# Another opening for a fused attention and mixture-of-experts kernel: two projection tiles first, weight groups centred beside the heads, zero products in TensorE's gaps

## What is computed

```python
qkv = jnp.einsum('bsh,oh->bso', x, w_qkv)            # x is already normalised
...
q = _layernorm(q, qn_g, qn_b)
k = _layernorm(k, kn_g, kn_b)
q = q * cos + _rotate_half(q) * sin
k = k * cos + _rotate_half(k) * sin
...
scores = jnp.einsum('bhqd,bhkd->bhqk', q, k) / jnp.sqrt(jnp.float32(D))
weights = jax.nn.softmax(jnp.where(causal, -jnp.inf, scores), axis=-1)
...
x = x + _layernorm(attention(_layernorm(x)), axis=-1)
x = x + _layernorm(experts(_layernorm(x)), axis=-1)
```

## Time and profile before

| | |
|---|---|
| median of 3 runs | 674.17 us (672.75 to 674.7) |
| the profiled execution's own time | 673.56 us |
| its span in the trace | 671.8 us |
| busy: PE, weight loads, DVE, ACT, POOL | 94%, 87%, 82%, 82%, 79% |
| mean granted clock of PE | 0.991 |

### The profile page before, as it was taken

How to read it: one execution, slowest core, us unless ns; L and a number is a source line. 1 busy time by engine, 2 the same in 40 slices (tenths; PEclk the granted TensorE clock), 3 DMA queues, 4 the chain that set the end, 5 groups by cost and what they waited for, 6 DMA issues and landing times.

```text
span 671.8 us, 15617 instructions
## 1 busy us (share of the span) xinstructions
PE 631.1 (94%) x4506; PEld 586.9 (87%) x4506; DVE 549.9 (82%) x1912; ACT 551.3 (82%) x2105; POOL 530.5 (79%) x601
## 2 busy tenths in 40 slices
PE   5879999999999999999999999999789989999993
PEld 5657899999999999999999999999678889999991
DVE  3989999898898889899898999979878755555466
ACT  3589999999999999999999999999787536666633
POOL 3698898999899899989989998999757424666664
PEclk9999999999999999999999999999899999999997
DMA  8001306997740000000000000000526033444173
GB/s 328 33 0 33 104 1 198 335 335 209 4 47 1 1 1 1 1 1 2 1 1 1 1 1 2 1 1 25 160 101 229 33 90 111 128 130 119 67 265 125
DMA packets 51122, 54.27 MB, mean 81 GB/s; under 512 B 19840, under 2 KB 42752, under 8 KB 50912
## 3 DMA queue, kind: packets, MB, share of 16 engines
q1 hardware_dynamic: 47632, 43.90, 23.6%
q0 software_dynamic: 3408, 9.38, 3.7%
HBM read 23.83 MB, written 29.51 MB: 79 GB/s over the span
## 4 chain that ended last, share of the span: by engine, by line
PE 75%; DVE 9%; POOL 5%; issue 4%; ACT 4%; DMA 2%; POOLq 0%; SPq 0%; ACTq 0%; DVEq 0%
PE pQ L470 8%; PE pQ L471 8%; PE pQ L472 8%; PE pPO L576 5%; PE pPO L470 5%; PE pPO L472 5%; PE pPO L471 5%; PE pT L548 4%; PE pSS L470 3%; PE pA L470 3%; PE pA L471 3%; PE pA L472 3%; PE pSS L471 2%; PE pSS L472 2%; POOL xs L2076 2%
## 5 line engine op out<-in xcount | busy, mean ns | idle before, releaser
L1002 ACT ACTIVATE P<-P,nmx 128x128 f32<-128x128 f32 (+1 forms) x256 | 118.8, 491 | 1.0 <-DVE nmx L1445 1.0
L470 PE MATMUL pQ<-W 128*128 128x512 f32 (+2 forms) x334 | 116.1, 347 | 2.4 <-DVE W L1359 1.2
L471 PE MATMUL pQ<-W 128*128 128x512 f32 (+2 forms) x334 | 111.6, 334 | 0.0
L472 PE MATMUL pQ<-W 128*128 128x512 f32 (+2 forms) x334 | 111.3, 333 | 0.0
L1982 POOL TENSOR_TENSOR ropes<-ropes 128x640 f32<-128x640 f32 x63 | 99.3, 1576 | 13.7 <-DVE ropes L1422 13.4
L1010 ACT ACTIVATE P<-P,rinv 128x128 f32<-128x128 f32 (+1 forms) x256 | 105.8, 481 | 2.1 <-DVE rinv L1451 2.1
L1992 POOL TENSOR_TENSOR ropes<-ropes 128x640 f32<-128x640 f32 x63 | 99.6, 1580 | 4.9
L470 PE MATMUL pPO<-W 128*128 128x256 f32 (+1 forms) x323 | 95.3, 295 | 5.6 <-DVE W L1460 3.9
L987 ACT ACTIVATE ropes<-pQ 128x128 f32<-128x128 f32 x320 | 88.4, 303 | 9.7 <-PE pQ L472 9.7
L471 PE MATMUL pPO<-W 128*128 128x256 f32 (+1 forms) x323 | 92.0, 285 | 0.0
L472 PE MATMUL pPO<-W 128*128 128x256 f32 (+1 forms) x323 | 91.8, 284 | 0.0
(11 more groups left out here) (272 smaller groups left out, 2170.5 us busy)
## 6 DMA issues: line engine op xcount, KB each, us to landing
xs<-stage SPq DMA_DIRECT2D x1, 17550.0 KB, 58.4
...
```

Of the source, the lines that this page charges most:

```text
L470: e.matmul(out, lh, rh, start=start, stop=False, skip_group_check=True)
L471: e.matmul(out, lh, rl, start=False, stop=False, skip_group_check=True)
L472: return e.matmul(out, ll, rh, start=False, stop=stop, skip_group_check=True)
L1002: a = e.activation(P[:, z, span(t)], P[:, z, span(t)], ACT.Exp, bias=nmx[:, z, t:t + 1], scale=-1.0, accum_out=sums[:, z, t:t + 1])
```

## The change

- SP's queue: the identity and centring matrices and the first half of weight group 0 are fetched first, then `X` (tokens of batch 0), then the second half, then the gains `gb` (before: `X`, matrices, first half, `gb`, second half). The tables `cs` and everything after keep their places.
- PE: `keep_running(n)` issues n products of a zeroed 128x128 tile with itself into `pT`: 8 at the very start, 2 and 3 around `centre(1)`, 5 before `qkv(0, 0)`, and 8 before `qk_T(1, 0)`. DVE zeroes the tile first (`still`).
- The four projections of units 0 and 1 stand together, unit 1 in `pSS` and unit 0 in `pQ`; then `centre(2)` into `pPO` and `centre(3)` into `pQ`; then `qk_T(1, ·)`, `qkv(2, 0)`, `qk_T(0, ·)`, `qkv(2, 1)`, `centre(4)`, `scores(0)`, `qkv(3, ·)`. The second round of transpositions of units 0 and 1 uses `pA`.
- `centre(5)`, `(6)`, `(7)` stand in steps 8, 9 and 10, beside `scores(0)`, `(1)`, `(2)`; all of them and `centre(4)` use `pPO`, so each waits for the `wq_lo` of the one before (`WFREE`).
- Unit 1's end on DVE is cut in two, `rope_add(1)` and `rope_scale(1)`, with `wq_lo(2)` between; it no longer waits for unit 0. `ln1_stats(1)` moves from step 6 to step 9. POOL computes unit 1's roots before it scales unit 0, and leaves out one small operation for batch 0.

```diff
-QFIRST = 6
-CENTRE = {0: [2], 1: [3], 3: [4, 5], 5: [6], 6: [7]}
+OPEN = 8
+CENTRE = {8: [5], 9: [6], 10: [7]}
+SPLIT = {8: [5], 9: [6], 10: [7]}
+WFREE = {2: 2, 4: 3, 5: 5, 6: 6, 7: 7}
+ROUND = {(1, 0): 0, (1, 1): 1, (0, 0): 2, (0, 1): 3}
...
-        pW = [pSS[:, 0:GW], pPO[:, 0:GW]]
+        pW = [p[:, 0:GW] for p in (pSS, pPO, pPO, pQ, pPO, pPO, pPO, pPO)]
+        pQu = [pSS if u == 1 else pQ for u in range(NU)]
+        pTr = [pA if i in (1, 3) else pT for i in range(2 * NU)]
...
-            e.dma_start(X[:, 0:2, :], x_d[:, 0:2, :]).then_inc(s_dx[0], 16)
             e.dma_start(const[:, 0:256], const_d[:, 0:256]).then_inc(s_dconst, 16)
             e.dma_start(raw_q[0][:, 0, :], wqkv_d[:, 0, 0, :]).then_inc(s_dwq[0], 16)
+            e.dma_start(X[:, 0:2, :], x_d[:, 0:2, :]).then_inc(s_dx[0], 16)
+            e.dma_start(raw_q[0][:, 1, :], wqkv_d[:, 0, 1, :]).then_inc(s_dwq[1], 16)
             e.dma_start(gb[:, :, :], gb_d).then_inc(s_dgb, 16)
-            e.dma_start(raw_q[0][:, 1, :], wqkv_d[:, 0, 1, :]).then_inc(s_dwq[1], 16)
...
-                if i >= 2:
-                    e.wait_ge(s_wqlo, i - 1)
+                if i == 3:
+                    e.wait_ge(s_v, 1)
+                elif i >= 2:
+                    e.wait_ge(s_wqlo, WFREE[i])
...
+            def keep_running(n):
+
+                for i in range(n):
+                    e.matmul(pT[:, 0:128], still, still, start=True, stop=True, skip_group_check=True)
+
+            e.wait_ge(s_still, 1)
+            keep_running(8)
             centre(0)
+            keep_running(2)
+            centre(1)
+            keep_running(3)
             ln1_T(0)
-            centre(1)
-            for s in range(WOVEN):
+            keep_running(5)
+            qkv(0, 0)
+            qkv(0, 1)
+            qkv(1, 0)
+            qkv(1, 1)
+            centre(2)
+            centre(3)
+            keep_running(8)
+            qk_T(1, 0)
+            qk_T(1, 1)
+            qkv(2, 0)
+            qk_T(0, 0)
+            qk_T(0, 1)
+            qkv(2, 1)
+            centre(4)
+            for s in range(OPEN, WOVEN):
                 n = s - LS
                 tu, tr = divmod(s - 5, 2)
...
+                if s == OPEN:
+                    qkv(3, 0)
+                    qkv(3, 1)
                 for i in CENTRE.get(s, []):
                     centre(i)
```

More of the change, by code:

```diff
@@ L109, in is_head, with stats_step, rnd @@
     return 0 <= s - LS - lag < NHEAD
+def stats_step(s):
+    return 0 if s == 9 else s // 16 if s > 16 and s % 16 == 6 and s // 16 + 1 < NB else None
+def rnd(u, r):
+    return ROUND.get((u, r), 2 * u + r)
 def span(t):
@@ L164, in program @@
         cs = p_flat[:, 4 * D:8 * D].rearrange("p (v t d) -> p v t d", v=2, t=2)
+        still = part(p_flat, 8 * D, D)
         ss = sb("ss", [128, 2, 5])
@@ L526, in qkv @@
                     e.wait_ge(s_hT, b + 1)
-                if u > 0 and y == 0:
+                if u == 1:
+                    e.wait_ge(s_wqlo, 1)
+                elif u == 2:
+                    e.wait_ge(s_wqlo, 4)
+                elif u > 2 and y == 0:
                     e.wait_ge(s_t2, 2 * u - 1)
-                if u > 0 and y == 1:
+                elif u > 2:
                     e.wait_ge(s_v, u)
@@ L535, in qkv @@
                         e.wait_ge(s_wqlo, 2 * g + kk + 1)
-                    p = mm3(pQ[:, c0:c1], [hT[:, b % 2, i, kk, t * 128:t * 128 + 128] for i in range(2)],
+                    p = mm3(pQu[u][:, c0:c1], [hT[:, b % 2, i, kk, t * 128:t * 128 + 128] for i in range(2)],
                             [WQ[:, g, i, kk, c0:c1] for i in range(2)], kk == 0, kk == 1)
@@ L1178, in ffn @@
                     last_apply(p)
+            wq_hi(0)
+            wq_hi(1)
             e.wait_ge(s_dgb, 16)
             e.activation(gb[:, 0:2, :], gb[:, 0:2, :], ACT.Copy, scale=float(D) ** -0.5).then_inc(s_gain, 1)
-            wq_hi(0)
             ln1_hi(0)
-            wq_hi(1)
-            for s in range(WOVEN):
+            rope(0, 0)
+            rope(0, 1)
+            spread(0)
+            rope(1, 0)
+            rope(1, 1)
+            wq_hi(2)
+            wq_hi(3)
+            spread(1)
+            qT_hi(1, 0)
+            qT_hi(1, 1)
+            rope(2, 0)
+            qT_hi(0, 0)
+            qT_hi(0, 1)
+            rope(2, 1)
+            wq_hi(4)
+            rope(3, 0)
+            for s in range(OPEN, WOVEN):
                 n = s - LS
                 tu, tr = divmod(s - 5, 2)
-                if QFIRST <= s <= 2 * NU:
+                if s <= 2 * NU:
                     rope((s - 1) // 2, (s - 1) % 2)
@@ L1200, in _ @@
                     logit_lo(fb)
-                if 0 < s < QFIRST:
-                    rope((s - 1) // 2, (s - 1) % 2)
-                if 0 <= tu < NU:
+                if 2 <= tu < NU:
                     qT_hi(tu, tr)
@@ L1212, in _ @@
                     ln2_apply(fb)
-                for i in HI.get(s, []):
+                for i in SPLIT.get(s, []):
                     wq_hi(i)
-                if s in (2, 3):
-                    spread(s - 2)
                 if s in WOS:
@@ L1772, in ffn @@
                         last_add_tile(p, t)
+            e.memset(still, 0.0).then_inc(s_still, 1)
             ln1_stats(0)
+            wq_lo(0)
             ln1_apply(0)
-            wq_lo(0)
+            wq_lo(1)
             ln1_lo(0)
-            wq_lo(1)
             scale_tables1()
-            for s in range(WOVEN):
+            rope(0, 0)
+            rope(0, 1)
+            bias_table1()
+            rope(1, 0)
+            rope(1, 1)
+            rope_add(1)
+            wq_lo(2)
+            rope_scale(1)
+            wq_lo(3)
+            qT_lo(1, 0)
+            qT_lo(1, 1)
+            rope(2, 0)
+            qT_lo(0, 0)
+            qT_lo(0, 1)
+            rope(2, 1)
+            wq_lo(4)
+            soft_max(0)
+            rope(3, 0)
+            for s in range(OPEN, WOVEN):
                 n = s - LS
@@ L1795, in _ @@
                     logit(fb)
-                if 0 < s < QFIRST:
+                if 2 <= tu < NU:
+                    qT_lo(tu, tr)
+                if s <= 2 * NU:
                     rope((s - 1) // 2, (s - 1) % 2)
-                if 0 <= tu < NU:
-                    qT_lo(tu, tr)
-                if QFIRST <= s <= 2 * NU:
-                    rope((s - 1) // 2, (s - 1) % 2)
-                if is_head(s, 0):
+                if is_head(s, 0) and n > 0:
                     soft_max(n)
-                if s % 16 == 6 and s // 16 + 1 < NB:
-                    ln1_stats(s // 16 + 1)
+                if stats_step(s) is not None:
+                    ln1_stats(stats_step(s) + 1)
                 if 0 <= fb < NB - 1:
@@ L2146, in _ @@
             e.tensor_tensor(TB[:, 0, 3:5, :], TB[:, 0, 3:5, :], ctmp[:, 0, :, :], ALU.add).then_inc(s_tab_p, 1)
-            for s in range(WOVEN):
-                if s == 2:
-                    rope(0)
-                if QFIRST <= s <= 2 * NU and (s - 1) % 2 == 1:
+            rope(0)
+            rope(2)
+            for s in range(OPEN, WOVEN):
+                if s <= 2 * NU and (s - 1) % 2 == 1:
                     rope((s - 1) // 2)
-                if s % 16 == 6 and s // 16 + 1 < NB:
-                    ln1_root(s // 16 + 1)
+                if stats_step(s) is not None:
+                    ln1_root(stats_step(s) + 1)
                 fb, fs = divmod(s - LATE - 15, 16)
```

94 lines of the change are left out of this document (50 added, 44 removed).

## The result

The changed kernel took 677.89 us as the median of 7 runs (676.58 to 678.73), beside 674.17 (671.81 to 675.55) for 7 runs of the kernel before: 3.7 us more, and a ratio of 1.0056 with a 95% interval of [1.0038, 1.0074]. Its profiled execution is one of 677.89 with a span of 675.9, so 2.0 lie outside the span; before it was 673.56 and 671.8, which leaves 1.8. The mean granted clock went from 0.991 to 0.987.

What follows compares the result with a forecast made beforehand. It took DVE (60 to 80), then PE as the bound, the opening as a chain across engines. Waits 1.5 plus clock 1.5 on 673.56 gave 676.6, or 677.2 from the median; it said 676.9 us, range 672.0 to 679.0.

Steps and rivals of the forecast that it cites:

- The start: Opening up to `rope(0,0)`: earlier weights and zero products start it at 14.4 against 15.66, a gain of 1.2.
- DVE up to `wq_lo(3)`: DVE's stream from `rope(0,0)`: `wq_lo(3)` ends at 24.8 and `rope_scale(1)` at 23.9, the lead growing to 1.8.
- the meetings with POOL: DVE and POOL sharing SBUF ports in the opening: taken as 0 extra, at most about 1.0.
- Where the lead goes: Between `qk_T(1,0)` and `rope(5,0)`: PE idles 3.8, DVE waits 2.0 and 2.6; `rope(5,0)` at 47.3, a loss of 1.5.
- The clock: PE's clock falls in the 3.8 gap; about 3 us then run at half speed, costing 1.5 (0 to 1.7).
- `centre(7)`: PE reaches it at 39.9 and waits for `wq_lo(6)` until 42.4, a wait of 2.5.
- From 45 on: Behind the opening: DVE, then PE, is full, so the loss goes to the end nearly whole, nothing made good.
- port meetings and clock together: Rival for DVE and POOL in the opening: port blocking adds 1.0 to the clock loss, 677.9 to 678.5; chance 0.15.
- the lead is kept: Rival at `centre(7)`: `wq_lo(6)` ends before PE asks, so the kernel is faster, 672 by the median; chance 0.20.
- The zeros don't raise the clock: Rival at the start: centrings stay at 2.4 each, first projection 1.0 later, 677.9 (676 without the fall); chance 0.05.

Runs made afterwards that it cites:

- e1: The changed kernel with 26 zero products instead of 8 between `centre(3)` and `qk_T(1,0)`; ratio to the kernel before 1.0026.
- e9: The changed kernel with 26 zero products in PE's gap, batch 1's statistics before `rope(2,0)`, and `wq_lo(6)` ahead of `soft_max(1)`; ratio to before 1.0001.
- e7: The kernel before with only the new fetches, the start's zero products and the first pieces in the changed order; ratio to before 0.9988.
- e10: The changed kernel with `bias_table1()` moved right behind `scale_tables1()`, ahead of `rope(0,0)`; ratio to before 1.0046.
- e5: The changed kernel with `wq_lo(6)` put ahead of `soft_max(1)` and `ln1_stats(1)` in DVE's step 9; ratio to before 1.0024.
- e2: The changed kernel without any zero products, at the start or in the gaps; ratio to before 1.0073.
- e3: The changed kernel with `ln1_stats(1)` moved from step 9 to ahead of `rope(2,0)` on DVE; ratio to before 1.0032.
- e4: The changed kernel with unit 2's first projection ahead of unit 1's transpositions, ACT and DVE reordered likewise; ratio to before 1.0074.
- e8: e4 with 17 zero products in place of 8 in PE's gap; ratio to before 1.0020.
- e6: The changed kernel with e3, e4 and e5's edits, 17 zero products, and `qkv(2,1)` ahead of `qk_T(0,0)`; ratio to before 0.9989.

## Why the prediction was right

The forecast was 676.9 in 672.0 to 679.0, and 677.89 came. Two waits of PE and a fall of its clock were forecast, and all three are there. But the range was wide, and the loss came out larger than the forecast had it: 3.7 between the medians for 2.7. At the landmark the miss is plain: `rope(5,0)` was forecast at 47 to 49, with 47.3 and 1.5 for the clock making 48.8, and came at 49.91. The table goes through the sum. The two stretches "with the clock up" are measured in e1 and, within 0.01, in e9; the last one is the changed kernel's own, as its clock was up there.

| term | forecast | measured | missing |
|---|---|---|---|
| start of `rope(0,0)` | 14.4 | 14.59 | 0.2 |
| `rope(0,0)` to `rope(2,0)`, with the clock up | 13.3 | 13.73 | 0.4 |
| `rope(2,0)` to `rope(4,0)`, with the clock up | 10.9 | 11.10 | 0.2 |
| `rope(4,0)` to `rope(5,0)` | 8.7 | 8.87 | 0.2 |
| the clock behind the first gap | 1.5 | 1.6 | 0.1 |
| sum: `rope(5,0)` | 48.8 | 49.9 | 1.1 |

By its steps:

- **The start.** Forecast 4.8 for the weights, 11.6 for the first projection, 14.4 for `rope(0,0)`; they came at 4.62, 11.72 and 14.59. The clock was forecast to rise at about 6.1 and rose later: the first centring takes 2.39 whole, the second 1.28. Other profiles of the same start have the rise earlier and `rope(0,0)` up to 0.8 sooner, so the good agreement of this term is in part luck. e7 isolates the step: 0.9 at `rope(5,0)`, near the forecast gain of 1.2.
- **DVE up to `wq_lo(3)`.** Forecast to end at 24.8, measured 25.4 (24.43 + 0.95). The start was 0.2 later than forecast. The other 0.4 belongs to the term that I had set at 0 within 0 to 1.0, the meetings with POOL: 1.3 appeared at the bias table (16.73), and 0.8 was saved at the scaling (1.28 for 2.07). This is **the term of the sum that was mis-sized most**, at 0 for 0.4. The Trainium skill (SBUF — State Buffer, section "SBUF: two separate sides") holds that a DVE instruction with two SBUF inputs and GpSimd's block each other for a whole instruction. This trace and e10 agree: 1.3 of waiting beside an addition of 1.70, 1.2 beside one of 1.99. Beside POOL's root over five values, 1.19 long, the same two products took 0.49 (e7) and did not wait, so not every instruction of POOL holds DVE for its whole length. Its reading as a full 1.0 more was too much, because another meeting went away.
- **Where the lead goes.** Forecast a PE gap of 3.8 that ends with `rope_scale(1)`, measured 4.14 and that releaser. Forecast `rope(2,0)` at 27.7 with the clock up; e1, in which the clock stayed up, has 27.95.
- **The clock.** Forecast 1.5 (0 to 1.7) for half speed behind the gap. The stretch from `rope(0,0)` to `rope(4,0)` is 26.45 in the changed kernel and 24.83 in both e1 and e9: 1.6. The mechanism and the size hold.
- **`centre(7)`.** Forecast to wait 2.5; it waited 2.37, from 42.6 on (forecast 39.9, or 41.4 with the clock). e5, which moves only the work ahead of `wq_lo(6)`, makes the stretch to `rope(5,0)` 1.5 shorter. DVE's 2.6 of idle time before unit 4's transposes was measured as 2.60, and DVE's idle time from 25 to 45 rose from 3.6 to 7.2.
- **From 45 on.** Forecast that nothing is made good. The shift is 4.1 at `rope(5,0)` and 3.7 at 52, at 168 and at 286. So 0.4 is made good at once, and this, which no step foresaw, brought the median nearer to the forecast than the landmark is.

By time alone the outcome lies nearest to the rival *port meetings and clock together* (677.9); that rival had the mechanism right too, but at 1.0 where the rows give 0.4.

The rival *the lead is kept* failed at the point it named: `wq_lo(6)` did not end before PE asked. When that wait is mended (e5, e9), the kernel reaches 1.0024 and 1.0001, not the 0.997 of the rival. DVE's 2.6 of idle time before unit 4 stay in every version of the new order (2.60 to 2.62), which fits this; no run takes them away. *The zeros don't raise the clock* fell by e2 beside e1, e3 and e4.

What stays open: where the clock falls in the runs of e4 that have no profile, and why e1 and e8 lose less by their medians (1.8 and 1.3 us) than their profiled executions show at batch 5 (2.65 and 2.5). In the same way e6 is 1.6 ahead of the kernel before at batch 5 in its profile and e7 0.8, with the same median.
